# Widening the halves of steps 1 to 3 on VectorE in four copies instead of two, in a graph network kernel

## The chip, the cores and the metric

The kernel runs on one core of a Trainium2 chip. Its time is the device time of that core in microseconds, the median of several runs.

## The reference, cut to what matters

Four graph layers follow each other over 6,250 nodes of 64 features and 200,000 edges. The change lies in the first one, a gated graph network of four steps:

```python
def step(feat, _):
    transformed = jnp.einsum('nd,khd->knh', feat, W) + b[:, None, :]     # one message per node and edge type
    msgs = transformed[etypes, src]
    a = jax.ops.segment_sum(msgs, dst, num_segments=num_nodes)
    feat = _gru_cell(a, feat, w_ih, w_hh, b_ih, b_hh)
    return (feat, None)
feat, _ = jax.lax.scan(step, h, None, length=4)
```

The last layer needs, for each source node, the sum and the maximum of the 32 attributes of its edges:

```python
seg_sum = jax.ops.segment_sum(edge_attr, row, num_segments=N)
seg_max = jax.ops.segment_max(edge_attr, row, num_segments=N)
```

## The kernel before, in words

**The counts.** The sum over the edges is done as matmuls. An early stage writes a dense matrix of counts into HBM (`mat_d`, one byte per pair of a (source node, edge type) row and a target node, 6,272 columns for each type; rare counts that need rows of their own are in `ext_d`). Each step multiplies the messages with these counts. Step 0 also does other work on them (sums over the types, and a mask for later layers). Steps 1, 2 and 3 are alike, and they are the place of the change.

**Steps 1 to 3** (`contract_halves`). Each step runs over the columns in two halves of `HQ` = 3,136. A piece is 128 rows of counts by 3,136 columns; a step has `MPS` = 406 pieces, so the three steps have 1,218. SyncE's queue loads the pieces as bytes, two per transfer, into one of four raw buffers (line 736). An engine widens the bytes of a piece to fp32 into one of five buffers `full` (`WIDES`). TensorE multiplies it with the messages of the block in seven matmuls of 448 columns (line 858). `by_dve(m)` deals the pieces out: of five consecutive pieces two, `m % 5 in (1, 3)`, are widened by VectorE (lines 1459 and 1460, 487 pieces), and three by ScalarE in one instruction (line 1016, 731 pieces). TensorE's wait for a piece is on a count that its engine raises after the last copy (`s_hd` for VectorE, `s_ha` for ScalarE). The piece `m` may be widened when the piece `m - 5` has been used.

**VectorE's order** is written out by hand. In each of the 406 ticks of a step it widens a piece if it is VectorE's turn, finishes a message of the next block if one is due (`message`, lines 1425 to 1435), and does a part of the scan of edge attributes if one is due (`scanned`).

**The attributes.** Beside the steps GpSimd gathers the attributes of the 200,000 edges, sorted by source: 1,568 indirect DMAs (line 666), each of 128 rows of 128 bytes, in 32 slabs of 49. There are three slab buffers. VectorE scans a slab (lines 1541 to 1548, a running sum and a running maximum, in 16 portions on every second tick) at ticks that a table fixes (`slab_turns`), in turn with the widening. `scanned` with portion 0 waits until all 49 gathers of its slab have landed. ScalarE's queue then stores the slab. GpSimd also gathers, once in each step, seven tiles of messages for the rows in `ext_d` (line 610), at a place fixed in its order (`GATHERED`); VectorE waits for these in `message_extra` (line 1443).

Between two steps TensorE, ScalarE and VectorE compute the gates (`gates`, `grown`), seven groups of 448 columns.

Of the kernel before, what the change touches and what calls it, by code (L numbers as in the profile page):

```python
# [45 lines left out]
HQ = NP // 2  # L46
# [21 lines left out]
QW = 1568  # L68
# [74 lines left out]
def by_dve(m):  # L143

    return m % 5 in (1, 3)
# [151 lines left out]
def build(nc, x, src, dst, attr, etype, W0, b0, wih, whh, bih, bhh, W1g, a1, u3, W13, b13, W23, b23, out):  # L297
# [20 lines left out]
    def sems(st, *names):  # L318
        made_here = [nc.alloc_semaphore(n) for n in names]
        st.held += made_here  # L320
        return made_here
# [46 lines left out]
    with top:  # L368
# [40 lines left out]
        with Phase() as ph:  # L409
# [19 lines left out]
            s_ha, s_hd, s_hu, s_ws = sems(ph, *(t + n for n in ("halfact", "halfdve", "halfused", "unscaled")))  # L429
# [88 lines left out]
            sumW = QW // 4  # L518
# [31 lines left out]
            def half_ready(eng, m):  # L550


                u, at = PIECES[m][5:7]
                eng.wait_ge(s_lh[u % RAWS], 16 * (u // RAWS + 1))
                if m >= WIDES:
                    eng.wait_ge(s_hu, m - WIDES + 1)
                else:
                    eng.wait_ge(s_us, PPS)
                    eng.wait_ge(s_base, NB)
                return full[:, m % WIDES, :].bitcast(F32R), raw[:, u % RAWS, at * HQ:(at + 1) * HQ]  # L560
# [579 lines left out]
            def _(dve):  # L1140
# [148 lines left out]
                for j in range(NSG):  # L1289
                    lo, hi = j * SEG, (j + 1) * SEG  # L1290
                    own = slice(j, j + 1)
# [164 lines left out]
                def half_wide(m):  # L1456
                    if m < MPS * (STEPS - 1) and by_dve(m):
                        to, own = half_ready(dve, m)
                        dve.tensor_copy(to[:, 0:QW], own[:, 0:QW])  # L1459
                        dve.tensor_copy(to[:, QW:HQ], own[:, QW:HQ]).then_inc(s_hd, 1)  # L1460

                def lower_in(st, h):

# [114 lines left out]
                def grown(st):  # L1578
# [30 lines left out]
                    for j in range(NG):  # L1609
                        if j + 1 < NG:  # L1610
                            before(j + 1)
                        elif st + 1 < STEPS:
                            message(st + 1, 0)
                        after(j)
                        if st == 0 and j in (2, 4):
                            half_wide(j - 1)
# [18 lines left out]
                for st in range(1, STEPS):  # L1635
                    message(st, 1)
                    for i in range(MPS):
                        at = MPS * (st - 1) + i
                        if i == HALF_AT:
                            lower_in(st, 0)  # L1640
                        half_wide(at + LEAD)
                        if i in MADE:
                            message(st, MADE[i])
                        if i == EXTRA_TICK:
                            message_extra(st)
                        if st == 1 and i < NQ:
                            last_sums(i)
                        if at in SCANS:
                            scanned(*SCANS[at])
                    grown(st)  # L1650
# [780 lines left out]
```

## Time and profile before

| | us |
|---|---|
| median of 3 runs | 8936.63 |
| the three runs | 8867.32, 8936.63, 9012.96 |
| span of the profiled execution, first to last instruction | 6770.6 |
| steps 1 to 3 and the gates between them | about 2866 to 5403 of that span |

For the profiled execution the span is known, and not its own device time. The runs shown are longer than the span by some 2,100 to 2,240 us, which lie outside the first and the last instruction. Times on the trace count from the first instruction. Engines: PE is TensorE's matmuls, PEld its weight loads, DVE VectorE, ACT ScalarE, POOL GpSimd, SP SyncE. The page divides the span into 40 slices of 169 us; the three steps are slices 18 to 32:

```profile
DVE  9898986777764565677556776658755588888754
ACT  0000006999975677488788778977778848888765
POOL 0019777777777777588787788878888500000071
PEclk9655557888887778799899888989889965555588
DMA  9931006888855566499898898877877725555496
```

Each digit is a share in tenths: of an engine's time that was busy, of full speed for the clock, and of the DMA engines' time. In the slices of the steps no engine is busy all the time.

### The profile page before, as it was taken

The numbers are of one execution on the slowest core, as the hardware profiler recorded it, in microseconds if no ns is written. First come the engines' busy times: TensorE is split into PE (matmuls) and PEld (weight loads), VectorE is DVE, ScalarE is ACT, GpSimd is POOL, SyncE is SP. The second block draws the span as 40 slices with busy tenths as digits, with TensorE's granted clock in tenths as the row PEclk, the third lists the DMA queues.
The fourth block names the chain that finished last, engine by engine and source line by source line (L and its number), as shares of the span: only waits on it lengthen the run. The fifth ranks groups of instructions, "written<-read, shape, count | busy, mean of one in ns | idle before, by whom it ended". The sixth has DMA issues, their size and how long they took to land. (4 is left out here: it accounts for less than half of the span.)

```text
span 6770.6 us, 66189 instructions
## 1 busy us (share of the span) xinstructions
PE 4370.2 (65%) x21729; PEld 2790.3 (41%) x21729; DVE 4823.7 (71%) x9798; ACT 4457.4 (66%) x2943; POOL 4002.1 (59%) x3327
## 2 busy tenths in 40 slices
PE   0120117666654556488678787878877758888856
PEld 0110114333332233277566666766666621111245
DVE  9898986777764565677556776658755588888754
ACT  0000006999975677488788778977778848888765
POOL 0019777777777777588787788878888500000071
PEclk9655557888887778799899888989889965555588
DMA  9931006888855566499898898877877725555496
GB/s 411 428 151 0 0 11 229 298 300 293 297 214 201 206 221 241 152 309 302 230 271 252 244 298 256 303 248 272 280 250 275 246 112 227 218 214 226 168 325 214
DMA packets 523231, 1589.94 MB, mean 235 GB/s; under 512 B 148178, under 2 KB 207929, under 8 KB 493190
## 3 DMA queue, kind: packets, MB, share of 16 engines
q1 hardware_dynamic: 329082, 1408.51, 58.0%
q10 hardware_dynamic: 88332, 146.04, 6.4%
q0 software_dynamic: 105472, 31.16, 3.2%
q8 instruction: 171, 2.80, 0.2%
q14 instruction: 174, 1.43, 0.1%
HBM read 1046.14 MB, written 539.23 MB: 234 GB/s over the span
## 5 line engine op out<-in xcount | busy, mean ns | idle before, releaser
L623 POOL DMA_INDIRECT mat_d<-cT,idxT x1563 | 1776.4, 1137 | 937.7 <-issue 471.1
L1016 ACT ACTIVATE full<-ring 128x3136 fp32r<-128x3136 uint8 x731 | 1997.9, 2811 | 415.7 <-PE ps_all L858 243.2
L858 PE MATMUL ps_all<-full,TR 128*128 128x448 f32 x8232 | 1821.9, 380 | 322.3 <-DVE full L1460 190.3
L858 PEld LDWEIGHTS ps_all<-full,TR 128*128 128x128 f32 x8232 | 1582.8, 195 | 558.1 <-issue 173.8
L666 POOL DMA_INDIRECT two<-in_edge_attr,eid x1029 | 1293.7, 1257 | 361.4 <-issue 313.1
L809 PE MATMUL ps_all<-ring,T 128*64 128x448 f16 x8232 | 985.7, 404 | 678.5 <-ACT ring L1031 678.4
L809 PEld LDWEIGHTS ps_all<-ring,T 128*64 128x64 bf16 x8232 | 535.5, 125 | 1127.5 <-issue 514.1
L1030 ACT ACTIVATE ring<-ring 128x3136 uint16<-128x3136 uint8 x197 | 553.5, 2810 | 366.8 <-DMA ring<-mat_d 235.5
L666 POOL DMA_INDIRECT ring<-in_edge_attr,eid x539 | 680.9, 1263 | 164.3 <-issue 164.0
L1502 DVE SCALAR_TENSOR_TENSOR two<-two 128x392 f32<-128x392 uint16 x768 | 388.9, 564 | 545.4 <-DMA csum_d<-two 538.4
L1459 DVE CAST full<-ring 128x1568 fp32r<-128x1568 uint8 x487 | 481.9, 990 | 398.9 <-PE ps_all L858 205.4
L2175 POOL DMA_INDIRECT two<-seg_d,endI x49 | 88.0, 1797 | 1093.5 <-issue 1093.5
L761 PE MATMUL ps_all<-ident,two 128*128 128x128 f32 x448 | 108.7, 423 | 783.8 <-DVE two L1166 783.8
L1031 ACT ACTIVATE ring<-ring 128x3136 uint16<-128x3136 uint8 x197 | 551.6, 2800 | 0.0
L1460 DVE CAST full<-ring 128x1568 fp32r<-128x1568 uint8 x487 | 472.6, 970 | 0.0
L1954 ACT ACTIVATE L<-ps_all,bias 128x384 f32<-128x384 f32 x588 | 361.9, 624 | 99.5 <-PE ps_all L1908 99.5
L761 PEld LDWEIGHTS ps_all<-ident,two 128*128 128x128 f32 x448 | 87.4, 222 | 804.7 <-DVE two L1166 455.2
L1948 ACT ACTIVATE ps_all<-ad,as 128x384 f32<-128x384 f32 x588 | 374.3, 637 | 42.3 <-DVE bias L2074 14.7
L1165 DVE TENSOR_TENSOR two<-two 128x512 f32<-128x512 f32 x556 | 383.6, 690 | 2.6
L1166 DVE TENSOR_TENSOR two<-two 128x512 f32<-128x512 f32 x556 | 378.7, 681 | 0.0
L1048 ACT ACTIVATE X<-two 128x1568 uint8<-128x1568 uint16 x196 | 294.7, 1503 | 111.8 <-ACT X L1048 34.3
L1663 PE MATMUL ps_all<-two,HD 128*64 128x512 f32 (+1 forms) x832 | 351.8, 935 | 6.7 <-ACT L L1954 6.7
(418 smaller groups left out, 5497.5 us busy)
## 6 DMA issues: line engine op xcount, KB each, us to landing
ring<-mat_d SPq DMA_DIRECT2D x784, 784.0 KB
mat_d<-ring SPq DMA_DIRECT2D x98, 1568.0 KB, 39.5
csum_d<-two SPq DMA_DIRECT2D x192, 784.0 KB
two<-csum_d SPq DMA_DIRECT2D x32, 3136.0 KB, 10.1
base_d<-two SPq DMA_DIRECT2D x49, 1568.0 KB
TR<-two_d SPq DMA_DIRECT2D x282, 256.0 KB
C<-csum_d SPq DMA_DIRECT2D x17, 3136.0 KB, 10.1
C<-base_d SPq DMA_DIRECT2D x49, 800.0 KB, 11.8
```

Source lines behind the costliest of these rows:

```text
L623: pool.indirect_dma_start(mat_d, bass.IndirectOffsetOnAxis(idxT[:, col:col + 1], 0), cT[:, col:col + 1], None).then_inc(s_sc[g % 8], 16)
L666: pool.indirect_dma_start(slab[n % SLABS][:, c, 0:FA], None, attr, bass.IndirectOffsetOnAxis(eid[:, at:at + 1], 0)).then_inc(s_at[n % SLAB ...
L809: mm = pe.matmul(accs[h * D:(h + 1) * D, j, 0:GW], lhsT, ring[:, n % 6, h * HQ + j * GW:h * HQ + (j + 1) * GW], start=first, stop=True, sk ...
L858: mm = pe.matmul(accs[:, j, 0:GW], parts.bitcast(F32R), full[:, m % WIDES, j * GW:(j + 1) * GW].bitcast(F32R), start=first, stop=True, ski ...
L1016: act.activation(to, own, ACT.Copy).then_inc(s_ha, 1)
L1030: act.activation(to[:, 0, :], two[:, 0, :], ACT.Copy)
L1031: act.activation(to[:, 1, :], two[:, 1, :], ACT.Copy).then_inc(s_cva, 1)
L1165: dve.tensor_tensor(b[:, :, 0, :], a[:, :, 0, :], a[:, :, 1, :], ALU.min)
L1166: ended(dve.tensor_tensor(b[:, :, 1, :], a[:, :, 0, :], a[:, :, 1, :], ALU.max), [h])
L1459: dve.tensor_copy(to[:, 0:QW], own[:, 0:QW])
L1460: dve.tensor_copy(to[:, QW:HQ], own[:, QW:HQ]).then_inc(s_hd, 1)
L1502: ad = dve.scalar_tensor_tensor(CS[o % 2][:, h * sumW:(h + 1) * sumW], all4[:, at], 0.0, all4[:, at], ALU.mult, ALU.add, accum_out=rs[:, 4 ...
```

## The change

In steps 1 to 3 VectorE's pieces are widened by four copies of 784 columns each (`sumW` is `QW // 4` = 392) instead of two of 1,568. The count `s_hd` is raised by the last of the four. ScalarE's pieces, the shares of both engines and all else stay.

```diff
                 def half_wide(m):
                     if m < MPS * (STEPS - 1) and by_dve(m):
                         to, own = half_ready(dve, m)
-                        dve.tensor_copy(to[:, 0:QW], own[:, 0:QW])
-                        dve.tensor_copy(to[:, QW:HQ], own[:, QW:HQ]).then_inc(s_hd, 1)
+                        for k in range(4):
+                            cp = dve.tensor_copy(to[:, k * sumW * 2:(k + 1) * sumW * 2], own[:, k * sumW * 2:(k + 1) * sumW * 2])
+                        cp.then_inc(s_hd, 1)
```

## Rows read from the trace of the kernel before

**Rows 1.** The page: span, and each engine's busy time and instructions.

```profile
span 6770.6 us, 66189 instructions
...
PE 4370.2 (65%) x21729; PEld 2790.3 (41%) x21729; DVE 4823.7 (71%) x9798; ACT 4457.4 (66%) x2943; POOL 4002.1 (59%) x3327
```

**Rows 2.** Windows: stretch, length, busy PE, PEld, DVE, ACT, POOL, clock, DMA share, GB/s.

```profile
2866.00:3688.00 822.00, 663.62 (x2940) 560.50 (x2940) 551.51 (x1331) 679.26 (x263) 653.27 (x521) 0.91 0.92 281
...
3731.00:4554.00 823.00, 664.65 (x2940) 568.50 (x2940) 548.61 (x1320) 671.53 (x254) 657.85 (x513) 0.90 0.87 276
...
4596.00:5403.00 807.00, 650.69 (x2940) 558.91 (x2940) 540.45 (x1289) 662.76 (x251) 625.47 (x489) 0.91 0.81 277
...
4600.00:4800.00 200.00, 187.85 (x839) 152.29 (x839) 172.77 (x441) 178.26 (x65) 164.61 (x117) 0.98 0.92 324
```

**Rows 3.** VectorE's waits for GpSimd's gathers in step 1: us, times, longest.

```profile
DVE X L1443 <- DMA TRe<-two_d,exT: 24.6, 1, 24.6
...
DVE keep L1541 <- DMA ring<-in_edge_attr,eid: 9.5, 2, 6.6
DVE keep L1541 <- DMA two<-in_edge_attr,eid: 3.1, 1, 3.1
```

**Rows 4.** The same waits in step 2.

```profile
DVE keep L1541 <- DMA two<-in_edge_attr,eid: 59.0, 5, 15.9
...
DVE keep L1541 <- DMA ring<-in_edge_attr,eid: 26.6, 2, 14.7
```

**Rows 5.** The same waits in step 3.

```profile
DVE keep L1541 <- DMA two<-in_edge_attr,eid: 97.5, 6, 24.1
...
DVE keep L1541 <- DMA ring<-in_edge_attr,eid: 52.4, 3, 19.7
```

**Rows 6.** TensorE's waits for VectorE's pieces, 2850 to 5400 us.

```profile
PE ps_all L858 <- DVE full L1460: 190.3, 18, 19.3
```

**Rows 7.** GpSimd's gathers by line, 2800 to 5350 us: busy us, mean ns, idle.

```profile
L666 POOL DMA_INDIRECT two<-in_edge_attr,eid x1029 | 1293.7, 1257 | 361.4 <-issue 313.1 <-DMA csum_d<-two 48.0 <-DVEq L1576 0.3
L666 POOL DMA_INDIRECT ring<-in_edge_attr,eid x539 | 680.9, 1263 | 164.3 <-issue 164.0 <-DVEq L1576 0.3
```

**Rows 8.** The same groups in the window 4600 to 4800 us.

```profile
L666 POOL DMA_INDIRECT two<-in_edge_attr,eid x95 | 135.8, 1429 | 29.0 <-issue 29.0
```

**Rows 9.** Timeline: start us, us, instruction, idle before.

```profile
3403.65 0.94 POOL L666 DMA_INDIRECT ring<-in_edge_attr,eid  x1 [0.30 <-issue]
3404.90 1.60 POOL L666 DMA_INDIRECT ring<-in_edge_attr,eid  x1 [0.30 <-issue]
...
3405.41 0.98 DVE L1459 CAST full<-ring 128x1568 fp32r<-128x1568 uint8 x1 [2.27 <-DMA ring<-mat_d]
3406.30 0.98 DVE L1460 CAST full<-ring 128x1568 fp32r<-128x1568 uint8 x1
3406.81 1.28 POOL L666 DMA_INDIRECT ring<-in_edge_attr,eid  x1 [0.30 <-issue]
3407.20 0.30 DVE L1546 TENSOR_TENSOR_SCAN two<-keepM,state,two 128x49 f32<-128x49 f32 x1
3407.42 0.29 DVE L1548 TENSOR_TENSOR_SCAN two<-keep,state,two 128x49 f32<-128x49 f32 x1
...
3411.69 2.34 POOL L666 DMA_INDIRECT ring<-in_edge_attr,eid  x1 [0.30 <-issue]
...
3412.07 0.95 DVE L1459 CAST full<-ring 128x1568 fp32r<-128x1568 uint8 x1
3412.95 0.96 DVE L1460 CAST full<-ring 128x1568 fp32r<-128x1568 uint8 x1
```

**Rows 10.** Timeline of VectorE in step 0: eight additions of 784 numbers in a row.

```profile
2011.85 3.90 DVE L1483 TENSOR_TENSOR two<-ring 128x784 uint16<-128x784 uint16 x8
```

**Rows 11.** The page: the two widening copies, with busy us, mean ns, idle before.

```profile
L1459 DVE CAST full<-ring 128x1568 fp32r<-128x1568 uint8 x487 | 481.9, 990 | 398.9 <-PE ps_all L858 205.4 <-DMA ring<-mat_d 174.5 <-DVE idxT L1435 5.5
...
L1460 DVE CAST full<-ring 128x1568 fp32r<-128x1568 uint8 x487 | 472.6, 970 | 0.0
```

## The prediction

> **What bounds the kernel now.** I read the page first, for the share of each engine [rows 1], and then the windows of the three steps, because the edit touches nothing else. There TensorE, ScalarE and GpSimd are each busy about 80% of the time, VectorE 67%, and the DMA engines 0.92, 0.87 and 0.81 [rows 2]. None is at its limit, so the waits must tell. VectorE waits at the first portion of a slab for GpSimd's gathers, little in step 1 (9.5 + 3.1 us, and 24.6 us for the gathered messages) [rows 3], then 59.0 + 26.6 us in step 2 [rows 4] and 97.5 + 52.4 us in step 3 [rows 5]. That is 273 us in all. VectorE works in order, so the pieces that it should widen stand behind such a wait, and TensorE waits 190.3 us for them, up to 19 us at a time [rows 6]. GpSimd itself waits for almost nothing but its own issue: 1,568 gathers of 1.26 us, with 0.30 us of issue between them [rows 7]. 1568 x 1.56 = 2,446 us of the 2,537 us between 2866 and 5403. So the three steps are paced by GpSimd's chain, more in each step than in the one before. In step 1 the pace comes from the DMA engines.
>
> **Why a gather takes 1.26 us.** Undisturbed it takes 0.94 us. The timeline shows what lengthens it [rows 9]. The gather that starts at 3404.90 should end at 3405.84. A copy of VectorE runs from 3405.41 to 3406.39, and the gather ends at 3406.50, 0.11 us after that copy and inside the next one. The gather of 3406.81 starts inside a copy that ends at 3407.28 and ends at 3408.09, 0.81 us later. The gather of 3411.69 ends at 3414.03, 0.12 us after the second of two copies. So a gather needs something twice that a running copy withholds: once at its start (if it is held, it ends 0.81 us after the release) and once about 0.5 us in (if held, it ends 0.12 us after the copy's end). It can get in between two copies. Where VectorE is densest, at 4600 to 4800, the mean is 1.43 us [rows 8].
>
> **The change, part by part.**
>
> *Two more copies per piece.* No row shows a copy of 784 numbers. The nearest is the addition of 784, eight in 3.90 us: with 0.56 us for the last, (3.90 - 0.56) / 7 = 0.48 us from start to start [rows 10]. The copy of 1,568 takes 0.88 us from start to start and 0.97 us by itself [rows 9, 11]. A piece thus takes 0.88 + 0.97 = 1.85 us now and 3 x 0.48 + 0.56 = 2.00 us after, 0.14 us more before rounding, 0.07 us for each added copy. 487 pieces x 0.14 = 68 us on VectorE. Bounds: nothing at all, or the 0.22 us from start to start of a scan of 49 numbers, which is nearly all fixed cost [rows 9]: 974 x 0.22 = 214 us. I take 68, since the additions have the very size. Most of it lies beside the 399 us for which VectorE idles before its pieces [rows 11] and the waits for slabs. In the densest stretch VectorE is busy 173 of 200 us [rows 2] and has no such cover; that is about a quarter of the time, so I charge 17 us.
>
> *The gathers.* Copies cover 487 x 1.85 = 901 us of the 2,537, a share of 0.36. An early request that meets a copy waits half of it, less 0.13 us that the gather has in hand (0.94 - 0.81): 0.31 us for a period of 0.88 us, and 0.11 us for 0.48. A late request waits only beyond 0.31 us, as 0.43 us of the gather follow it anyway: on average (0.88 - 0.31)^2 / (2 x 0.88) = 0.18 us now, and (0.48 - 0.31)^2 / (2 x 0.48) = 0.03 us after. A gather held by the first copy of a piece meets the second one for certain and loses 0.19 us more, for half of those held; with short copies it does not. Now: 0.36 x (0.31 + 0.18 + 0.10) = 0.21 us. After, with a share of 0.38: 0.38 x (0.11 + 0.03) = 0.05 us. The measured hold is 1.26 - 0.94 = 0.32 us; the missing 0.11 us come from the scans and from gathers that fail to get in at a boundary, and these boundaries become more. So of the 0.16 us I take 0.12, and 0.08 to 0.17 as bounds. 1568 x 0.12 = 188 us off GpSimd's chain (125 to 267).
>
> *What reaches the end.* A wait that goes away is partly given back, as the next limit comes up. The fastest stretch does 839 matmuls in 200 us [rows 2]; at its pace a step's 2,940 take 200 x 2940 / 839 = 701 us. Step 1 runs at a DMA share of 0.92 already, the share of that fastest stretch, so of its 37 us of waits I take 20. Step 2 (823 us, waits of 86) gets 55, step 3 (807 us, waits of 150) gets 85; both stay above 701. Sum: 160 us, less than the 188 us of GpSimd. Late next is the DMA queue with the counts, then ScalarE, busy 663 to 679 us of each step [rows 2].
>
> Net: -160 + 17 = -143 us. Against the profiled span: 6770.6 - 143 = 6,628 us. Its device time is not given; the median of 8936.6 lies 2,166 us above the span, and I leave that untouched. 8936.6 - 143 = 8,794 us.
>
> **The rivals.**
>
> *Something else holds the steps* (chance 0.20). GpSimd gets faster, but the DMA engines or ScalarE take over at once in steps 2 and 3 as in step 1. For it: shares of 0.81 to 0.92. Against it: the stretch at 324 GB/s against 276 to 281 on average [rows 2]. Gain 0 to 80 us: about 8,897.
>
> *VectorE becomes the pace* (0.08). The pieces arrive later and TensorE waits for each. All 68 us count: 9,005. Against it: 67% busy.
>
> The Trainium skill, "VectorE: DVE Perf Modes", section on the TRN2 errata, speaks for this rival: every SBUF-source instruction pays a fixed price, 58 cycles at 0.96 GHz, and many small tiles pay it each time. As an estimate from that page, 974 x 0.06 = 59 us, and a forecast of 8,996 if nothing hid it. The rows give 0.07 us each.
>
> *The copies of one piece are not let go* (0.04), the one that ends slower. The place is the boundary between short copies, each of which starts before its forerunner has ended. If a gather gets in only after the fourth, an early request waits (2.00 / 2 - 0.13) = 0.87 us and a late one (2.00 - 0.31)^2 / 4 = 0.71 us: 0.38 x 0.87 + 0.62 x 0.38 x 0.71 = 0.50 us, and against the whole measured hold of 0.32 us that is 0.18 x 1568 = 280 us more, paid in full by the chain that sets the pace: 9,217. It decides from a mean hold above 0.32 us. Against it: the gather that ended at 3406.50 [rows 9].
>
> The Trainium skill, "SBUF — State Buffer", section "SBUF: two separate sides", speaks against this rival: VectorE in a two-port mode and GpSimd exclude each other for one instruction at a time, whoever starts first, and nothing there ties several instructions together. The page's "blocked until DVE-end + ~115 ns" leads to the same sum as the 0.11 and 0.12 us of the rows.
>
> *All of it reaches the end* (0.06). The hold falls by 0.17 us and all 273 us of waits go: 8,670.
>
> The forecast itself, 80 to 230 us less, has 0.62.
>
> **How the numbers follow.** Main case: 8,707 to 8,857 us, with 8,794 the likeliest. The range from 8,700 to 8,950 takes in the second case too and leaves out the two slower ones and most of the last, with some room for the scatter of medians. 2% is 179 us, about what a measurement of this kernel can tell from no change, as its three runs lie 1.6% apart. Faster by more: the last case and a third of the main one, 0.06 + 0.20 = 0.26. Slower by more: 0.04. Within: 0.70.
>
> **What would show it.** Mean of line 666 at about 1.14 us (1.0 to 1.18 right; 1.25 or more wrong); the start-to-start time of the copies at 0.48 us; waits at line 1541 down from 248 us to below 100; the windows of steps 2 and 3 shorter by more than step 1's; a DMA share near 0.9 in all three. If the gathers are faster and the windows are not, the first rival holds. I am wrong altogether if gathers get slower, or if the time outside the span moves by more than the steps do.

## The result: 6% slower, by 465 us

The changed kernel takes 9373.48 us (median of 4 runs, 9347.29 to 9415.06). The kernel before, whose median of 3 was 8936.63, stands at 8908.48 with a fourth run. Ratio of the runs 1.0642, 95% interval 1.0587 to 1.0698. The forecast was 8,794. Here and below medians are of all runs and ratios only of the fast ones, those within 1.5% of the quickest of their kernel, so a ratio a little off 1 can point the other way than its two medians.

The experiments show that two kinds of chip are behind these figures, and nothing below can be read without it. On some chips the kernel before takes 8,520 to 9,010 us in every run, on others 6,630 to 6,790. By its span of 6770.6 us the trace from which the prediction was made comes from a chip of the second kind, and the runs that set the median from one of the first; which chips these two were is not known. In the text "slow chips" and "quick chips" stand for these. The times of the change are those of a slow chip.

The page of the changed kernel, against [rows 1]:

```profile
span 9348.4 us, 67163 instructions
...
PE 4712.4 (50%) x21729; PEld 2874.9 (31%) x21729; DVE 4890.2 (52%) x10772; ACT 4459.4 (48%) x2943; POOL 3499.7 (37%) x3327
```

Its device time is 9350.1 us, 1.7 us above its span. So almost nothing lies outside the first and the last instruction, and the 2,166 us of before did not either (b_again, below, shows it for the kernel before).

Steps 1, 2 and 3 with their gates are these windows of the changed kernel (stretch, length, busy PE, PEld, DVE, ACT, POOL, clock, DMA share, GB/s):

```profile
4246.00:5553.00 1307.00, 740.09 (x3054) 590.94 (x3050) 602.37 (x1713) 700.06 (x287) 537.42 (x530) 0.76 0.61 177
5553.00:6868.00 1315.00, 758.38 (x3056) 600.74 (x3058) 596.64 (x1689) 685.81 (x279) 588.07 (x587) 0.75 0.57 175
6868.00:7959.00 1091.00, 724.93 (x3054) 584.90 (x3054) 589.80 (x1657) 676.44 (x277) 484.85 (x457) 0.81 0.61 205
```

and of the unchanged kernel on a slow chip (b_again, below):

```profile
4150.00:5381.00 1231.00, 736.82 (x3054) 589.09 (x3054) 580.73 (x1385) 698.68 (x288) 606.22 (x555) 0.77 0.64 188
5381.00:6405.00 1024.00, 708.05 (x3054) 576.33 (x3054) 574.32 (x1365) 684.14 (x280) 615.13 (x525) 0.83 0.72 223
6405.00:7339.00 934.00, 682.74 (x3054) 567.89 (x3054) 568.61 (x1335) 675.94 (x278) 636.30 (x521) 0.87 0.71 241
```

ScalarE is busy for the same time in both, 2,062 and 2,059 us, VectorE for 65 us more, and TensorE for 96 us more, at a granted clock of 0.76, 0.75 and 0.81 instead of 0.77, 0.83 and 0.87. Yet the steps take 3,713 us instead of 3,189, 524 us more. (The two traces are of different slow chips; a third trace of the kernel before, b_third, has 3,244, so the size is 470 to 524 us, and the 465 us between the medians of one comparison is the safer figure.) In between the engines idle. What for, the waits of the changed kernel tell (4160 to 7960 us: us in total, times, longest). VectorE, against [rows 3 to 5]:

```profile
DVE full L1460 <- remote: 887.5, 34, 55.3
```

and in b_again (4100 to 7340 us), the same kind of wait and those for the slabs:

```profile
DVE full L1459 <- remote: 373.0, 13, 56.1
...
DVE keep L1541 <- DMA two<-in_edge_attr,eid: 99.7, 6, 24.1
DVE keep L1541 <- DMA ring<-in_edge_attr,eid: 46.3, 5, 16.5
```

GpSimd in the changed kernel and in b_again:

```profile
POOL csum_d L658 <- DVEq L1577: 884.1, 8, 157.3
```

```profile
POOL csum_d L658 <- DVEq L1576: 624.5, 6, 145.1
```

TensorE in the changed kernel, against [rows 6]:

```profile
PE ps_all L858 <- issue: 473.8, 199, 18.7
```

VectorE's waits for gathers at the scan, 248 us in the trace of the prediction and 146 us in b_again, are gone from the list altogether. GpSimd is ahead and waits for VectorE, 884 us. It was so in part on a slow chip before the change already, with 624.5 us, against 19.9 us in the trace of the prediction: the change carries further what that kind of chip does anyway. VectorE's largest sum of waits is put down to "remote", for which the profile names no engine of the core, and TensorE's largest sum to "issue", where nothing that the profile shows was awaited (261.2 us in b_again, 7.8 us in the trace of the prediction). The gathers themselves, against [rows 7], did become shorter, by more than was predicted:

```profile
L666 POOL DMA_INDIRECT two<-in_edge_attr,eid x1029 | 1057.9, 1028 | 1988.5 <-DMA csum_d<-two 1377.8 <-issue 311.4 <-DMA seg_d<-two 299.2
L666 POOL DMA_INDIRECT ring<-in_edge_attr,eid x539 | 540.2, 1002 | 317.7 <-issue 163.1 <-DMA seg_d<-ring 154.7
```

### The profile page after: what moved, and what is told of

It is laid out like the page before. It is cut to its first block and busy times, and to the rows that moved or that the text cites. A ratio compares the mean times of both kernels' runs of the same rounds, so it can differ in the third digit from the quotient of the medians.

```text
span 9348.4 us, 67163 instructions
## 1 busy us (share of the span) xinstructions
PE 4712.4 (50%) x21729; PEld 2874.9 (31%) x21729; DVE 4890.2 (52%) x10772; ACT 4459.4 (48%) x2943; POOL 3499.7 (37%) x3327
## 5 line engine op out<-in xcount | busy, mean ns | idle before, releaser
L858 PE MATMUL ps_all<-full,TR 128*128 128x448 f32 x8232 | 1975.0, 395 | 1022.9 <-issue 473.8
L858 PEld LDWEIGHTS ps_all<-full,TR 128*128 128x128 f32 x8232 | 1644.1, 204 | 1346.9 <-issue 764.4
L623 POOL DMA_INDIRECT mat_d<-cT,idxT x1563 | 1659.8, 1062 | 948.8 <-issue 482.0
L809 PE MATMUL ps_all<-ring,T 128*64 128x448 f16 x8232 | 1151.4, 405 | 1386.1 <-issue 995.4
L666 POOL DMA_INDIRECT two<-in_edge_attr,eid x1029 | 1057.9, 1028 | 1988.5 <-DMA csum_d<-two 1377.8
L1460 DVE CAST full<-ring 128x784 fp32r<-128x784 uint8 x1948 | 978.3, 565 | 1460.5 <-remote 887.5
L809 PEld LDWEIGHTS ps_all<-ring,T 128*64 128x64 bf16 x8232 | 555.7, 123 | 1978.6 <-issue 1417.7
L666 POOL DMA_INDIRECT ring<-in_edge_attr,eid x539 | 540.2, 1002 | 317.7 <-issue 163.1
L1413 DVE TENSOR_TENSOR t<-ps_all,biasB 128x256 f32<-128x256 f32 x49 | 20.8, 424 | 1023.8 <-remote 922.8
L804 PE MATMUL ps_all<-Wt,two 64*128 64x256 f32 (+1 forms) x500 | 202.0, 515 | 280.7 <-DVE t L1425 136.1
```

The lines of the kernel that those rows point to most:

```text
L623: pool.indirect_dma_start(mat_d, bass.IndirectOffsetOnAxis(idxT[:, col:col + 1], 0), cT[:, col:col + 1], None).then_inc(s_sc[g % 8], 16)
L666: pool.indirect_dma_start(slab[n % SLABS][:, c, 0:FA], None, attr, bass.IndirectOffsetOnAxis(eid[:, at:at + 1], 0)).then_inc(s_at[n % SLAB ...
L809: mm = pe.matmul(accs[h * D:(h + 1) * D, j, 0:GW], lhsT, ring[:, n % 6, h * HQ + j * GW:h * HQ + (j + 1) * GW], start=first, stop=True, sk ...
L858: mm = pe.matmul(accs[:, j, 0:GW], parts.bitcast(F32R), full[:, m % WIDES, j * GW:(j + 1) * GW].bitcast(F32R), start=first, stop=True, ski ...
L1460: cp = dve.tensor_copy(to[:, k * sumW * 2:(k + 1) * sumW * 2], own[:, k * sumW * 2:(k + 1) * sumW * 2])
```

## What happens on a slow chip

The slices of the page show it at once. The kernel before on a slow chip (b_again), each slice 218 us:

```profile
PE   0110003111114667675484555766838886788866
...
POOL 0057775777773000001466443274874884000041
```

and on a quick one (b_fourth), each slice 166 us:

```profile
PE   0110116766667645687787887879877768888866
...
POOL 0007777777777776778787788878877400000080
```

While GpSimd scatters (its first block of 7) TensorE is mostly at 0 or 1 on the slow chip and soon at 6 on the quick one. The windows 1800 to 2000 us, slow chip first, then quick:

```profile
1800.00:2000.00 200.00, 38.30 (x72) 9.10 (x71) 0.00 (x0) 13.95 (x6) 155.34 (x144) 0.50 0.05 10
```

```profile
1800.00:2000.00 200.00, 142.77 (x1158) 76.59 (x1160) 150.20 (x423) 187.88 (x82) 155.50 (x147) 0.84 0.83 297
```

GpSimd does the same in both, 144 and 147 operations. On the slow chip TensorE does 72 matmuls instead of 1,158 and VectorE nothing. The traces of the two other slow chips have 71 (b_third) and 72 (tiny_more) in this window. The timeline there (start, us, instruction, idle before):

```profile
1900.21 1.10 POOL L623 DMA_INDIRECT mat_d<-cT,idxT  x1 [0.30 <-issue]
1901.34 0.53 PE L809 MATMUL ps_all<-ring,T 128*64 128x448 f16 x1 [2.27 <-issue]
1901.62 1.10 POOL L623 DMA_INDIRECT mat_d<-cT,idxT  x1 [0.30 <-issue]
1902.74 0.13 PEld L809 LDWEIGHTS ps_all<-ring,T 128*64 128x64 bf16 x1 [2.67 <-issue]
```

TensorE starts one instruction for each of GpSimd's, 0.02 to 0.03 us after that has ended (1900.21 + 1.10 = 1901.31, start 1901.34), every 1.40 us, and idles in between with nothing to wait for. In the steps the engines idle in stretches too, though there the matmuls don't start right behind a gather:

```profile
4952.60 0.53 PE L858 MATMUL ps_all<-full,TR 128*128 128x448 f32 x1 [1.57 <-issue]
...
4954.70 0.53 PE L858 MATMUL ps_all<-full,TR 128*128 128x448 f32 x1 [1.57 <-issue]
4955.66 0.95 POOL L666 DMA_INDIRECT two<-in_edge_attr,eid  x1 [0.30 <-issue]
...
4964.41 1.27 POOL L666 DMA_INDIRECT two<-in_edge_attr,eid  x1 [0.30 <-issue]
4964.59 0.98 DVE L1459 CAST full<-ring 128x1568 fp32r<-128x1568 uint8 x1 [51.11 <-remote]
```

Two matmuls are 2.10 us apart with 1.57 us of idle time. Gathers of 0.95 us follow each other every 1.25 us, none is held, and VectorE runs nothing for 51 us. Once VectorE copies, the gathers are held (1.27 us). I call this starving. Counted over all records of the traces in stretches of 20 us, those with fewer than 20 matmuls are 3 of 129 in the steps on the quick chip (the trace of the prediction), 41 of 159 on the slow one (b_again), and 61 of 185 with the change. The 20 more of them are some 400 us of the 524; where the 20 us begin moves each count by up to four.

**Theory D**: on slow chips the other engines starve while GpSimd issues indirect DMAs one upon the other undisturbed. VectorE's long copies disturb it, by holding the gathers, and so protect the others. Four short copies hold less, and the starving stretches grow. **Theory C** (the rival): 974 more instructions on VectorE cost the time by their number, or by the time that they keep VectorE busy. In the experiments the steps' length is from the first matmul of the gates of step 0 to that of step 3.

## The experiments

Each ran beside the kernel before on one chip; ratios are to that.

**b_again**: the kernel before, unchanged.

> The kernel before, unchanged, profiled once more. Its profiled execution spanned 6770.6 us while its timed runs took 8867 to 9013 us. Theory A (the four copies themselves slow steps 1 to 3): this profile spans 6,770 us again, and the 2,100 us lie outside the span. Theory B (the kernel has two ways of running, and the profile shown was the quick one): this profile spans about 8,900 us, its gathers of line 666 take about 1.03 us instead of 1.26, and its stage of sorting and step 0 is as slow as in the changed kernel.

8792.21 us, ratio 1.006 (0.998 to 1.014), span 8724.4 at 8726.16 us of device time. The usual time is inside the span. Steps 3,189 us, gathers 1.158 us on average and not 1.03.

**s3_four**: four copies in step 3 only.

```diff
-                        dve.tensor_copy(to[:, 0:QW], own[:, 0:QW])
-                        dve.tensor_copy(to[:, QW:HQ], own[:, QW:HQ]).then_inc(s_hd, 1)
+                        w = QW // 2 if m >= MPS * 2 else QW
+                        for k in range(HQ // w):
+                            cp = dve.tensor_copy(to[:, k * w:(k + 1) * w], own[:, k * w:(k + 1) * w])
+                        cp.then_inc(s_hd, 1)
```

> Four copies of 784 in step 3 alone, two of 1,568 in steps 1 and 2. Theory A (each added copy costs where it is run): a third of the added time, 8,908 + 155 = 9,063 us, with step 3 longer and steps 1 and 2 as before. Theory B (the cost comes from where later code lies, not from the copies): all or nothing of the 465 us, and the time is lost outside step 3 too.

8913.71 us, ratio 1.023 (1.006 to 1.041), about a third of the loss. Its step 3 takes 1,074 us against b_again's 934:

```profile
6453.00:7527.00 1074.00, 710.62 (x3056) 575.04 (x3058) 590.98 (x1659) 677.57 (x278) 549.13 (x492) 0.81 0.62 209
```

Steps 1 and 2 together take 2,252 us, against 2,255 in b_again and 2,231 in b_third, which both have two copies there. Step 3 of b_third takes 1,013 us, so the unchanged step scatters by 79 us, and the four copies add 60 to 140. Within this scatter the loss sits where the four copies are.

**one_copy** and **eight**: one copy of 3,136 numbers, and eight of 392.

```diff
-                        dve.tensor_copy(to[:, 0:QW], own[:, 0:QW])
-                        dve.tensor_copy(to[:, QW:HQ], own[:, QW:HQ]).then_inc(s_hd, 1)
+                        dve.tensor_copy(to[:, 0:HQ], own[:, 0:HQ]).then_inc(s_hd, 1)      # one_copy
+                        for k in range(8):                                                # eight
+                            cp = dve.tensor_copy(to[:, k * sumW:(k + 1) * sumW], own[:, k * sumW:(k + 1) * sumW])
+                        cp.then_inc(s_hd, 1)
```

> One copy of 3,136 numbers for each of VectorE's pieces, so 487 instructions fewer than before. Theory A (the number of VectorE instructions costs): 465 us for 974 more, so 230 us less than before, about 8,680 us. Rival (the hold of the gathers costs, as the prediction had it): gathers longer and the time 100 to 300 us more than before.

> Eight copies of 392 numbers per VectorE piece, 2,922 instructions more than before. Theory C (count, 0.5 us each): about 8,900 + 1,400 = 10,300 us. Theory D (unheld gathers): the gathers are at 1.02 us with four copies and cannot go below 0.94, so only 100 to 300 us beyond the change: 9,500 to 9,700 us.

one_copy: 8704.91 us, 1.005 (0.998 to 1.012). eight: 9388.47 us, 1.094 (1.061 to 1.126). With the gathers' mean and the steps' length: one copy 1.293 us, 3,117; two 1.158, 3,189; four 1.019, 3,713; eight 0.997, 3,856. So the shorter the gathers, the longer the steps, on slow chips, but only four and eight copies stand clear of the scatter: the same two copies took 3,189 us in b_again and 3,244 in b_third. One copy holds the gathers most, and no gain of the whole is shown: its median is 62 us below that of the kernel before (8766.53), its ratio says 1.005. Neither of its expectations came, 230 us less or 100 to 300 us more. eight is 670 us above the kernel before on its chip (8718.56), 205 more than the change in its own comparison, as theory D had it, though below the absolute range.

**tiny_more**: as many more instructions as in the change, but the long copies stay.

```diff
-                        dve.tensor_copy(to[:, 0:QW], own[:, 0:QW])
+                        dve.tensor_copy(to[:, 0:16], own[:, 0:16])
+                        dve.tensor_copy(to[:, 16:32], own[:, 16:32])
+                        dve.tensor_copy(to[:, 32:QW], own[:, 32:QW])
```

> Four copies per VectorE piece as in the change, but of 16, 16, 1,536 and 1,568 numbers: the same 974 further instructions, while the two long copies go on holding GpSimd's gathers. Theory C (count: each VectorE instruction costs about 0.5 us in these steps): as slow as the change, about 9,370 us. Theory D (short copies let the gathers go faster, and while GpSimd issues indirect DMAs one after another undisturbed, the other engines hardly get to issue): near before, 8,770 to 8,900 us, gathers of 1.15 us.

8697.77 us, 1.006 (0.997 to 1.015); steps 3,169 us, gathers 1.148. VectorE is busy for 1,793 us of the steps, as long as in the changed kernel (1,789) and 70 us longer than in b_again (1,724). Theory C falls: neither the 974 more instructions nor VectorE's added busy time is to be seen in the kernel's time. What counts is that the long copies are cut up.

**four_paced** and **two_paced_all**: GpSimd is interrupted. four_paced is the change with a pause ahead of each gather; two_paced_all the kernel before with it ahead of each gather (line 666) and each scatter (line 623).

```diff
+            pace = sb(ph, "pace", [P, 128])
+            paced = count(3)
...
+                def pause():
+
+                    pool.memset(pace[:, :], 0.0).then_inc(s_z, 1)
+                    pool.wait_ge(s_z, next(paced))
```

> The changed kernel, with a memset of 128 numbers and a wait for it before each of GpSimd's 1,568 gathers, so that they follow each other at 1.5 us or more, not 1.25. Theory D: the long stalls of the other engines in steps 1 to 3 vanish or shrink although GpSimd has more to do; the time falls below the change's 9,370 by 300 us or more. Theory C, or the view that GpSimd's chain sets the pace: the same or slower, as 1,568 x 0.3 = 470 us are added to that chain.

> The kernel before, with the same pause before each of the 1,568 gathers and before each of the 1,563 scatters of the earlier stage. Theory D: the slow stretches of the sorting and of step 0 go too, and the time comes near the 6,770 us of the one quick execution, at most 7,800 us. Rival: GpSimd's chains get longer by up to 900 us and the time rises to 9,200 us or more.

four_paced: 8400.42 us, 0.981 (0.958 to 1.003) where the change has 1.064, and some 970 us less than it, of which some 190 are the chip's (8718.56 for the kernel before against 8908.48). Yet GpSimd has more to do. two_paced_all: 7541.57 us, 0.878 (0.863 to 0.893). The pause ahead of the scatters cures the stretch before the steps as well: they start at 3167 us instead of 4150. Both ran on one slow chip, and in the steps they have the same pause, so their steps compare two copies with four where the starving is stopped (two_paced_all, then four_paced):

```profile
3167.00:6156.00 2989.00, 2082.35 (x9164) 1729.19 (x9163) 1757.42 (x4083) 2061.02 (x843) 2479.93 (x3174) 0.85 0.72 230
```

```profile
4122.00:7011.00 2889.00, 2083.01 (x9164) 1733.50 (x9162) 1880.84 (x5057) 2063.77 (x842) 2383.59 (x3171) 0.86 0.75 237
```

Here the four copies make the steps 100 us shorter, on a slow chip and by one trace each (four_paced_all has 2,885 us on a quick one), with gathers of 1.112 instead of 1.181 us (0.069 x 1,568 = 108 us of GpSimd's chain). VectorE's waits for slabs are back, 518 us in four_paced. So the chip alone doesn't turn the sign of the change; GpSimd's uninterrupted chain does.

**few_two, few_four, four_paced_all, two_paced_short** came to a quick chip, where the kernel before took 6664.56 us in the median of 6 runs (6638.61 to 6764.54). That was the surprise of the study: the same kernel 24% quicker.

```diff
                        # few_two, few_four
+                        if c:
+                            continue
...
-                        dve.wait_ge(s_at[n % SLABS], 16 * SLAB * (n // SLABS + 1))
+                        dve.wait_ge(s_at[n % SLABS], 16 * (n // SLABS + 1))
                        # four_paced_all: the change and pause() at both places
                        # two_paced_short: as two_paced_all, with
+            pace = sb(ph, "pace", [P, 16])
```

> The kernel before, with only one of the 49 gathers of each slab of attributes issued (32 instead of 1,568); the rest of the slab holds whatever was there, so the attributes' sums and maxima are not those of the reference. Theory D (TensorE, ScalarE and VectorE hardly issue while GpSimd issues gathers one upon the other): steps 1 to 3 fall from the 3,189 us of the kernel before to 2,550 us or less, though VectorE and TensorE do the same work; the whole falls by the same 650 us and more, to about 8,100. Rival (the steps are long for a reason of their own, such as the counts' transfers or the chip's clock): steps 1 to 3 stay above 3,000 us.

> The same omission (one gather of 49 per slab), with the four copies. Theory D: the change costs nothing without the gathers: steps 1 to 3 within 70 us of few_two, which is VectorE's own price of 974 x 0.07 us. Rival (four copies cost VectorE, TensorE or the transfers something by themselves, whatever GpSimd does): steps 1 to 3 longer than few_two by most of the 524 us that the change costs in the full kernel.

> The four copies, with a memset of 128 numbers and a wait for its end ahead of each of the 1,568 gathers and 1,563 scatters. Theory D: with the pause in place the hold by VectorE's copies protects nothing any more, so the change is worth what the prediction's sum gave it or nothing: within 2% of two_paced_all, 7,400 to 7,650 us. Rival (the four copies hurt through something that the pause doesn't cure): 7,541 plus most of the 470 us that the change costs, about 8,000.

> The kernel before with the same pause, but with a memset of 16 numbers instead of 128, so that GpSimd is held up less by its own work while it still waits for the end of an instruction of its own. If what cures is that GpSimd's issue is interrupted at all, this is as good as two_paced_all or better by what the memsets save, 7,300 to 7,600 us. If what cures is the length of the pause, the time lies between: about 8,000 to 8,700 us.

few_two 6441.07 us (0.970, 0.966 to 0.974), steps 2,376; few_four 6459.65 (0.972, 0.968 to 0.977), steps 2,398; four_paced_all 7397.83 (1.113, 1.107 to 1.119); two_paced_short 7140.79 (1.075, 1.072 to 1.078). Where nothing starves a pause only costs, 476 us even if short. For the starving these runs say nothing, as their chip has none; so all but four_paced_all were repeated.

**after_again**: the changed kernel; it came to the same quick chip.

> The changed kernel as it is, beside the kernel before on one chip. The kernel before took 8,767 us on one chip and 8,719 on a second, but 6,665 us on a third, in all its runs there. Theory D, now with the chips in it (only on some chips do the other engines starve while GpSimd issues gathers undisturbed): where the kernel before takes about 8,700, the change costs 6% again; where it takes about 6,700, nothing starves, the prediction's sum applies, and the change gives 50 to 150 us, a ratio of 0.978 to 0.993. Rival (the four copies cost something that has nothing to do with starving): slower on either chip, above 1.02.

6609.70 us against 6646.85, ratio 0.9952 (0.9938 to 0.9966): the change is 37 us quicker there, by little but beyond the spread, and less than the 50 to 150 us that theory D expected. The rival, a cost on either chip, falls.

**b_third** and **b_fourth**: the kernel before again, for a trace beside it.

> The kernel before, unchanged, for a trace of it beside after_again. Theory D, where this chip runs it in about 6,650 us: gathers of 1.25 to 1.28 us on average (after_again: 1.195), and steps 1 to 3 some 30 to 60 us longer than after_again's 2,545 us, so that the 37 us by which the change is quicker there are all in steps 1 to 3. Where it takes about 8,700 us again, its gathers average 1.16 us and its steps about 3,190 us, as in b_again. Rival: the gathers are as short as after_again's, and the 37 us come from elsewhere.

> The kernel before, for a trace beside after_again if this is the chip that runs it in about 6,650 us: gathers of 1.25 to 1.28 us there, steps 1 to 3 some 30 to 60 us above after_again's 2,545. On another chip as b_again: gathers of 1.16 us, steps near 3,200, span near 8,700.

b_third met a third slow chip (8716.15 us, where the kernel before had 8722.22; steps 3,244, gathers 1.149). b_fourth met a second quick one: 6643.99 us, 1.0005 (0.999 to 1.002), span 6631.7. It is set beside after_again in the next section.

**few_two_b, few_four_b, two_short_b**: the same kernels as few_two, few_four and two_paced_short, now on a slow chip (the kernel before 8618.58 us, 5 runs).

> The two copies, with one gather of 49 per slab (the attributes' results are not the reference's), once more, since few_two ran on the chip that runs the kernel before in 6,665 us. Theory D, on a chip that takes about 8,700 for it: steps 1 to 3 fall from 3,189 to within 60 us of few_two's 2,376; the time before them, with its 1,563 scatters, stays as long as it is (the gates of step 0 at about 4,150 us). Rival (these chips are slow in the steps by themselves): steps 1 to 3 near 3,189.

> The four copies, with the same omission. Theory D: without the gathers the change costs nothing on these chips either, within 1% of few_two_b. Rival: it keeps most of its 6%.

> The kernel before with the short pause (memset of 16 numbers) ahead of each gather and scatter, on a chip that starves. Theory D, if it is the interruption that cures: as on the other chip, 7,100 to 7,250 us, and so the best version there. If it is the length of the pause: between 7,541 and 8,700.

few_two_b 7905.64 us (0.925, 0.910 to 0.940), few_four_b 7932.81 (0.926, 0.918 to 0.934). The windows of their steps, two copies and four:

```profile
4163.00:6537.00 2374.00, 2034.06 (x9164) 1683.26 (x9166) 1717.54 (x4083) 2057.61 (x843) 114.56 (x92) 0.95 0.85 279
```

```profile
4159.00:6545.00 2386.00, 2031.33 (x9162) 1684.17 (x9162) 1781.49 (x5057) 2056.60 (x843) 114.20 (x92) 0.94 0.85 277
```

Without most gathers the slow chip does the steps in 2,374 us, like the quick one (2,376), at a clock of 0.95, and the change costs 12 us in them instead of 524. The scatters before them were left in, and that stretch stayed as long as it was. So on slow chips 815 us of the steps come with the gathers, against 198 on a quick one (2,574 - 2,376), and nearly the whole cost of the change with them. two_short_b: 7194.47 us, 0.838 (0.829 to 0.848), the quickest that was measured on a slow chip. The same kernel took 7140.79 us on the quick one, with steps of 2,836 us against 2,865: with the short pause the two kinds of chip are 54 us apart, where without it they are about 2,000 apart. Its timeline, at the place shown above:

```profile
1900.04 1.15 PE L817 MATMUL ps_all<-ring,T 128*64 128x448 f16 x8
...
1900.26 0.13 POOL L581 MEMSET pace<- 128x16 f32 x1
1900.66 0.96 POOL L630 DMA_INDIRECT mat_d<-cT,idxT  x1 [0.28 <-issue]
...
1901.50 2.04 PE L817 MATMUL ps_all<-ring,T 128*64 128x448 f16 x15 [0.32 <-issue]
...
1902.02 0.97 POOL L630 DMA_INDIRECT mat_d<-cT,idxT  x1 [0.28 <-POOL pace L581]
```

From one scatter to the next it is 1.36 us (1902.02 - 1900.66), no more than the 1.40 above, and yet TensorE issues 23 matmuls beside them. In this stretch it isn't GpSimd's rate that counts. The first of the two scatters ends at 1900.66 + 0.96 = 1901.62. Between two DMAs it now has 0.40 us (1902.02 - 1901.62) with an instruction of its own and a wait for it, where it had 0.30 us. Whether the length or the wait does it, these runs don't separate.

**four_short**: the four copies with the short pause; it came to a quick chip (the kernel before 6648.82 us).

> The four copies with the short pause (memset of 16 numbers) ahead of each gather and scatter; the two copies with it took 7,141 and 7,194 us on two chips. With the starving cured, the prediction's sum applies: gathers shorter by 0.06 to 0.12 us (1.18 before), GpSimd's chain sets the pace at 1,568 x 1.66 us and gives 90 to 190 us, so 6,980 to 7,100 us. Rival (a faster GpSimd comes nearer to starving the others again): 7,200 or more.

7087.84 us, 1.066 (1.063 to 1.068), 53 us less than two_paced_short, with gathers of 1.150 instead of 1.176 us. So the four copies help where GpSimd's chain sets the pace and nothing starves, by somewhat over half of the least gain that was expected (the two kernels ran on two quick chips, whose medians for the kernel before are 16 us apart), and with gathers shorter by 0.026 us where 0.06 to 0.12 were expected. It wasn't run on a slow chip; there four_paced against two_paced_all speaks for the same.

## Why the prediction was wrong, by its steps

**Step "I leave that untouched" failed first, and hid the rest.** The prediction took the 2,166 us between span and median as lying outside the first and last instruction. They lie inside: 8726.16 us of device time, span 8724.4 in b_again. The profile that was shown belongs to another kind of chip than the times. What differs between b_again and b_fourth are 1,458 us before the steps (their start at 4150 against 2692), 615 us in them (3,189 against 2,574) and 19 us behind them. Its own sign of being wrong, "the time outside the span moves by more than the steps do", looked at the right place, but by itself the gap doesn't turn the sign of the change: the steps did that. A gap of a quarter of the time that no row explains was a sign that the rows weren't of the runs to be forecast, and it needed a case with a chance of its own.

**"The three steps are paced by GpSimd's chain" and the term of -160 us gave the wrong sign.** They hold on quick chips only. On slow chips the other engines nearly stop in stretches in which GpSimd runs free. There the gathers did get shorter (1.158 to 1.019 us) and VectorE's waits for slabs did go (146 us to none), as the sum wants it, and the steps got 524 us longer instead of 160 shorter. The prediction counted the hold as pure loss. It had no rival in which the hold is of use; its slower rivals, VectorE as the pace and copies not let go, are not what made the loss (few_four_b and tiny_more; gathers shorter on average, not longer). Its sign for the first rival, faster gathers without shorter windows, did appear, but not for that rival's reason: the DMA engines were less busy (0.57 to 0.61 instead of 0.64 to 0.72), not at their limit.

**Two more copies per piece: right.** VectorE's busy time on a quick chip rose by 72 us (4832.6 in b_fourth, 4905.0 in after_again), against 68, and four copies take 1.97 us, against 2.00. With few gathers the steps grew by 22 us on a quick chip (few_four against few_two) and by 12 on a slow one, against 17 charged.

**The gathers' hold** on a quick chip, b_fourth against [rows 7]:

```profile
L666 POOL DMA_INDIRECT two<-in_edge_attr,eid x1029 | 1297.8, 1261 | 360.9 <-issue 313.0 <-DMA csum_d<-two 47.6 <-DVEq L1576 0.3
L666 POOL DMA_INDIRECT ring<-in_edge_attr,eid x539 | 671.8, 1246 | 164.3 <-issue 163.7 <-DVEq L1576 0.6
```

and after_again:

```profile
L666 POOL DMA_INDIRECT two<-in_edge_attr,eid x1029 | 1221.5, 1187 | 360.6 <-issue 313.0
L666 POOL DMA_INDIRECT ring<-in_edge_attr,eid x539 | 652.8, 1211 | 164.3 <-issue 164.0 <-DVEq L1577 0.3
```

The mean over both fell from 1.256 to 1.195 us, by 0.06 and not by the 0.12 of the sum: 96 us off GpSimd's chain instead of 188. The trace tells which part failed. Gathers of 1.3 to 2.0 us fell from 283 to 82, the way the sum went. But those above 2.0 us did not: 140 before, 155 after. The sum had it that a held gather gets in between two short copies. Often it does not (GpSimd, then VectorE, after_again):

```profile
2771.52 2.81 POOL L666 DMA_INDIRECT ring<-in_edge_attr,eid  x1 [0.30 <-issue]
2774.63 2.46 POOL L666 DMA_INDIRECT ring<-in_edge_attr,eid  x1 [0.30 <-issue]
```

```profile
2771.54 1.97 DVE L1460 CAST full<-ring 128x784 fp32r<-128x784 uint8 x4
...
2774.30 1.97 DVE L1460 CAST full<-ring 128x784 fp32r<-128x784 uint8 x4
```

The four copies end at 2773.51 and 2776.27, the gathers 0.82 us later each time (2774.33 and 2777.09). They were held through all four. Of the gathers that overlap four copies or more, 151 took over 2 us and 170 took 1.3 us on average, so in about half of these cases the rival "the copies of a piece are not let go" is true. What decides between the halves I can't say. The rival's price, a mean hold above 0.32 us, didn't come, as the other gathers got shorter: 1.195 less 0.94 is 0.26 us. The Trainium skill, "SBUF — State Buffer", section "SBUF: two separate sides", has GpSimd and VectorE exclude each other for one instruction at a time; it ties no instructions together, and the prediction held this against the rival. It doesn't say who goes first at a boundary between two copies. The measurement decides: in 151 of these 321 cases the gather took over 2 us although such boundaries lay within it.

**What reaches the end.** On the quick chip VectorE's waits for slabs, against [rows 3 to 5], went from (b_fourth)

```profile
DVE keep L1541 <- DMA two<-in_edge_attr,eid: 160.4, 12, 25.9
DVE keep L1541 <- DMA ring<-in_edge_attr,eid: 88.4, 7, 19.7
```

to (after_again)

```profile
DVE keep L1542 <- DMA two<-in_edge_attr,eid: 121.7, 11, 22.2
...
DVE keep L1542 <- DMA ring<-in_edge_attr,eid: 55.9, 5, 13.5
```

that is 71 us less, and not below 100. TensorE's waits for VectorE's pieces, 203.2 us in b_fourth, are 147.1, and those for ScalarE's rose from 111.6 to 129.0: part was given back to the next limit, as expected. The steps went from 2,574 to 2,545 us: step 1 from 866 to 881, step 2 from 866 to 843, step 3 from 841 to 820, so only steps 2 and 3 gained, as forecast, and step 1 lost instead of giving its 20. So 96 us off the chain, 71 off the waits, some 17 back for the copies, 29 in the steps and 37 in the median. The mechanism that the prediction described exists, with a quarter of the size that was forecast (37 of 143 us), and shows in the time only where nothing starves. By its size it lies within the price of the first rival, 0 to 80 us, and below the main case, 80 to 230.

**Open.** Why the other engines can't issue on slow chips while GpSimd issues indirect DMAs isn't settled: no row names a resource. Nor is it known what sets the two kinds of chip apart. In the starving stretches cause and effect go round (an idle VectorE holds no gather, and an unheld gather starves VectorE). few_two_b and two_short_b show that the circle breaks at GpSimd's end; tiny_more against the change shows that it turns on the copies' length. That a long copy protects by holding a gather, and not by something else that goes with its length, is the reading that fits all runs, but no run shows it by itself.

## What to carry to other kernels

Before a sum is made, compare the profile's span with the times to be forecast. If they differ by more than the runs do among themselves, the trace is of another case, and every row needs a second reading. A hold or a wait that looks like pure loss may be what keeps a faster engine from starving the rest: where GpSimd issues many small indirect DMAs, look in the timeline for TensorE instructions that start one by one, each right behind one of these DMAs or far apart, with "issue" as their only wait. Where that is seen, a memset of 16 numbers and a wait on it between the DMAs gave 16%; where it isn't, the same pause cost 7.5%, so it must be measured on the chips in use.

## What the runs showed of the hardware that was not expected

The same kernel takes 8,619 to 8,792 us (medians) on three chips and 6,644 to 6,665 us on two, and no run of either kind came near the other. On the three, TensorE issues one instruction per 1.40 us beside back-to-back scatters, 71 or 72 matmuls in 200 us against 1,158. A memset and a wait between the scatters, with 0.40 instead of 0.30 us between them, at about the same rate, bring it back: 1,090 matmuls in the same 200 us of two_short_b. A gather can be held through four successive copies of VectorE, 2.81 us instead of 0.94.
